# Attention scores on half of the array's rows: both halves beside each other, in four groups of four matmuls

## The reference, cut to what matters

```python
x = x + _L0_xattn_ref(_layernorm(x), ctx_1024, Wq, Wk, Wv, Wp, bp)   # x: (32, 256, 256), ctx: (32, 120, 256)
x = x + _L0_ffn_ref(_layernorm(x), ...)
# in _L0_xattn_ref, q = split(x @ Wq), k = split(y @ Wk), v = split(y @ Wv), 16 heads of 16:
attn = jnp.einsum('bhid,bhjd->bhij', q, k) * SCALE
attn = jax.nn.softmax(attn, axis=-1)
out = jnp.einsum('bhij,bhjd->bhid', attn, v)
...
return out @ Wp + bp
```

## Time and profile before

| what | value |
|---|---|
| median of 2 runs | 975.79 us (974.56 to 977.03) |
| the profiled execution, its own time | 970.46 us |
| its span | 968.7 us |
| PE, DVE, ACT, POOL busy, share of the span | 88%, 77%, 53%, 61% |
| mean granted clock of TensorE | 0.941 |

### The profile page before, as it was taken

How to read it: one execution, slowest core, us unless ns; L and a number is a source line. 1 busy time by engine, 2 the same in 40 slices (tenths; PEclk the granted TensorE clock), 3 DMA queues, 4 the chain that set the end, 5 groups by cost and what they waited for, 6 DMA issues and landing times. The chain is left out here.

```text
span 968.7 us, 20968 instructions
## 1 busy us (share of the span) xinstructions
PE 848.8 (88%) x6115; PEld 727.1 (75%) x6115; DVE 742.9 (77%) x1659; ACT 510.7 (53%) x929; POOL 594.6 (61%) x562
## 2 busy tenths in 40 slices
PE   8799999999999999998611149999999999999995
PEld 6578888878888888886501137989999999999985
DVE  5588888888888888876598856988777777777642
ACT  4555565556655665565165107465555555555531
POOL 4266666677666766666342255588887776775345
PEclk9999999999999999999755559999999999999998
DMA  5466566566665665554141033466666556665333
GB/s 173 162 226 213 195 213 221 201 199 213 226 204 195 211 225 201 195 189 143 65 145 44 8 104 118 136 198 171 165 168 162 157 159 162 159 174 149 97 72 43
DMA packets 129508, 156.49 MB, mean 162 GB/s; under 512 B 22448, under 2 KB 104624, under 8 KB 129344
## 3 DMA queue, kind: packets, MB, share of 16 engines
q1 hardware_dynamic: 104064, 113.05, 35.9%
q0 software_dynamic: 15616, 25.70, 12.3%
q10 hardware_dynamic: 9792, 17.31, 4.9%
HBM read 74.93 MB, written 26.28 MB: 104 GB/s over the span
## 5 line engine op out<-in xcount | busy, mean ns | idle before, releaser
L583 DVE TENSOR_REDUCE NM<-bank 128x4 f32<-128x480 f32 x256 | 155.4, 649 | 60.6 <-PE bank L741 60.5
L414 ACT ACTIVATE PT<-bank 120x512 f32<-120x512 f32 x256 | 142.8, 603 | 36.6 <-PE bank L766 35.4
L342 POOL TENSOR_SCALAR XN<-X,mv,rstd 128x256 f32<-128x256 f32 x124 | 150.9, 1226 | 14.2 <-POOL rstd L337 13.3
L1656 PE MATMUL bank<-W2H,HH 128*128 128x256 f32 x512 | 144.8, 283 | 2.0 <-issue 2.0
L1658 PE MATMUL bank<-W2H,HL 128*128 128x256 f32 x512 | 143.6, 280 | 0.0
L1657 PE MATMUL bank<-W2L,HH 128*128 128x256 f32 x512 | 143.5, 280 | 0.0
L1117 POOL DMA_INDIRECT out_dram<-C,IO x60 | 111.3, 1855 | 50.7 <-issue 31.0
L1385 DVE TENSOR_TENSOR HL<-hf,HH 128x512 fp32r<-128x512 f32 x128 | 87.3, 690 | 49.8 <-ACT HH L1540 49.1
L766 PE MATMUL bank<-QX,KX 128*120 128x256 f32 x512 | 110.0, 307 | 9.4 <-DMA QX<-NMT 5.7
L541 DVE RECIPROCAL RR<-RC 128x256 f32<-128x256 f32 x64 | 111.5, 1743 | 6.3 <-DMA RC<-PVS 6.3
L1535 ACT ACTIVATE hf<-bank,B 128x512 f32<-128x512 f32 x128 | 87.9, 687 | 40.6 <-PE bank L1658 34.9
(11 more groups left out here) (192 smaller groups left out, 1888.4 us busy)
## 6 DMA issues: line engine op xcount, KB each, us to landing
QX<-QH ACTq DMA_DIRECT2D x64, 256.0 KB
W<-w1T_dram SPq DMA_DIRECT2D x16, 1024.0 KB, 5.5
W<-w2T_dram SPq DMA_DIRECT2D x16, 1024.0 KB, 5.8
X<-x_dram SPq DMA_DIRECT2D x32, 256.0 KB, 3.2
QX<-QL SPq DMA_DIRECT2D x32, 256.0 KB
XB<-x_dram SPq DMA_DIRECT2D x32, 256.0 KB, 2.8
RC<-PVS SPq DMA_DIRECT2D x64, 128.0 KB, 2.1
OC<-PVS SPq DMA_DIRECT2D x64, 128.0 KB, 2.3
```

What stands on the lines that cost most here:

```text
L342: ins = pool.tensor_scalar(dst[:, t, :], src[:, t, :], mv[:, t, 0:1], rstd[:, t:t + 1], ALU.subtract, ALU.mult)
L414: act.activation(PT[u][0:M, HE * k:HE * (k + 1), :], score_bank(b, k // 2)[k % 2][0:M, :], ACT.Exp, scale=SCALE) \
L583: dve.tensor_reduce(NM[u][:, t, :].rearrange("p (f n e) -> p n e f", n=HN, e=HE)[:, n, :, :], smax_bank[q % 2][:, 0:4 * M].rearrange("p (e ...
L1656: pe.matmul(o, wh, xh, start=first, stop=False)
```

## The change

`scores(n)` now runs for n = 0 to 3. Each call issues four matmuls: for each of two heads e, both halves f, on partitions 0 to 63 and 64 to 127 of `KX` and `QX`, the first into one bank, the second into the other. It waits once, until both banks have been read. The semaphore of half f is raised at the matmul of e = 1. The order of TensorE's step is rewritten around the four calls. ScalarE's code is the same.

```diff
-            def scores(k):
+            def scores(n):
                 b, u, j, live = batch(i, c, 0)
                 if live:
-                    n, f = k // HALVES, k % HALVES
-                    if k == 0:
+                    if n == 0:
                         pe.wait_ge(max_moved[u], 16 * (j + 1))
-                    wait(pe, exp_ready, NX * b + (k - HALVES * (2 if n > 0 and known(b) and b == B - 1 else 1) + 1))
+                    wait(pe, exp_ready, NX * b + HALVES * (n - (1 if n > 0 and known(b) and b == B - 1 else 0)))
                     for e in range(HE):
-                        ins = pe.matmul(score_bank(b, n)[f][0:M, e * S:(e + 1) * S], KX[u][:, n, f, e, :],
-                                        QX[u][:, HE * n + e, :], start=True, stop=True)
-                    ins.then_inc(score_done, 1)
+                        for f in range(HALVES):
+                            rows = slice(HP * f, HP * (f + 1))
+                            ins = pe.matmul(score_bank(b, n)[f][0:M, e * S:(e + 1) * S], KX[u][rows, n, f, e, :],
+                                            QX[u][rows, HE * n + e, :], start=True, stop=True)
+                            if e == HE - 1:
+                                ins.then_inc(score_done, 1)
...
             scores(0)
-            scores(1)
             values()
             if first == -1:
                 warm_up(WARM[2])
+            max_scores(0)
+            scores(1)
+            max_scores(1)
+            rows2()
             scores(2)
-            max_scores(0)
-            scores(3)
-            max_scores(1)
-            scores(4)
-            rows2()
-            scores(5)
             rows()
             if last == 3:
                 turn_logits(1, 0, EARLY)
             max_scores(2)
-            scores(6)
             max_scores(3)
-            scores(7)
+            scores(3)
             weigh(0)
             weigh(1)
```

## The result

| what | before | after |
|---|---|---|
| median | 975.79 us (2 runs) | 1002.34 us (999.33 to 1005.35, 2 runs) |
| ratio | | 1.028, 95% interval 1.023 to 1.033 |
| the profiled execution, its span | 970.46, 968.7 us | 1005.35, 1003.6 us |

A forecast was written before the change was run, and what follows sets the result against it. In the edited stretch ACT's exponentials and their handover were taken to set the pace, though PE is busiest overall. 0.57 us a step over 31 steps gives 17.7 us, 975.79 to about 994 us; range 989 to 1013 us.

The forecast's parts named there:

- handover: From the end of a pair's last exponential through the next score matmuls to the next exponential: ACT idle 0.65 us.
- The round: One scores(n) and its pair of exponentials: 1.09 us of exponentials plus 0.65 us between pairs, 1.74 us.
- the 0.94 us: PE time saved per step as sixteen score matmul slots of 0.12 us become eight; forecast to end in PE's waits.
- the changes of tiling: Seven more switches a step around the score groups, each bounded between nothing and 0.2 us, mostly falling into waits.
- The step "scores(0)": First score group, behind the router's matmuls: 0.09 us of drain, exp(0) moving from 205.68 to 205.70.
- The step "scores(1)": Second score group: PE arrives about 206.78, exp(1) ends 206.79, exp(2) starts at 207.44 instead of 207.07.
- The path to the weighing: From exp(4) at 209.18 through scores(3) to weigh(0) at 210.77, which PE reaches 0.57 us later than before.
- 31 of the 32 steps have this form: Attention steps: each 0.57 us longer, 17.7 us in all; the last sequence, with four score banks, put at nothing.
- forecast A: Halves run beside each other, exponentials' round sets the pace: 0.45 to 0.75 us a step, 990 to 999 us, chance 0.70.
- rival B: Row tiles don't run beside each other, four slots per group: 34 to 37 us slower, 1010 to 1013 us, chance 0.15.
- Rival C: Switch to row tiles dearer than 0.2 us, felt around scores(0): 25 to 28 us slower, 1001 to 1004 us, chance 0.12.
- Rival D: PE's work is the price and waits cost nothing: 29 us gained, 947 us, chance 0.03.

The follow-up runs named there:

- The wait alone: Kernel before, order and full rows kept, each score call waiting until both banks of the pair are read: 1008.33 us, ratio 1.034, step 14.94 us.
- the cut exponentials: Half of each exponential left out in both kernels, 256 of 512 columns read: changed kernel 981.89 us, kernel before 969.39 us.

## Why the prediction was right, and where it was off

- **Sign and cause: right.** ACT's round of a pair and its handover set the pace, PE's saving was used up. The wait alone (1.14 us a step) and the cut exponentials (0.51 us more gained than in the kernel before) show it.
- **The round: right.** 1.74 us from the earlier trace rows; measured 1.76, and 1.79 where PE came late; 1.74 twice with max_scores(0) moved.
- **Where the 0.94 us went: in part wrong.** "The 0.94 us that it saved are in its waits", and of the changes of tiling "it matters little, as most switches fall into a wait". Seven of them cost 0.94 + 0.33 = 1.27 us, more than was saved, so PE's own work grew from 13.41 to 13.74 us. The sum along ACT's rounds came out all the same, as the changes ahead of the third and fourth group end before the exponentials do. With no wait for ACT at all the change would still be slower, by an estimated 0.33 us a step.
- **The step "scores(0)": too small.** I gave it 0.02 us on the assumption that a drain behind the router's matmul takes 0.10. The router's last matmul starts at 210.26 + 0.97 - 0.26 = 210.97, the scores' load at 211.16, 0.19 later, and exp(0) comes 0.10 later on average (the 0.18 of the one step have 0.08 of the projection's ups and downs in them).
- **The step "scores(1)": too small by 0.03 on average**, 0.05 in the step shown. "PE's margin here is all but nothing" was right, and it was used up: the load of max_scores(0), whose call waits for transfers, begins at 212.56, only when the values' last matmul has streamed.
- **The path to the weighing: right**, 1.56 us from exp(4) to the weighing's load, as foreseen (209.18 to 210.74).
- **Sum.** 0.57 us a step forecast, 0.69 measured, 17.7 against 21.4 us for 31 steps. "31 of the 32 steps have this form" left out the fill: about 6 us more lie in the first two steps and the sixth to eighth. Hence 994 forecast and 1002.3 measured, on the side of 2% that I gave 0.52. The step of 0.69 us lies in forecast A's own range of 0.45 to 0.75; the time lies outside its 990 to 999 us. That it is inside the whole range is luck in part: the upper end was set by rival B, which is out.
- **Rival B** (no rows beside each other) is out: a group's 0.50 us are 0.10 of load, one slot of 0.12 and one matmul of 0.28, so the halves run together. **Rival C** was right in its place, PE's margin ahead of scores(1), and wrong in its reason: a change cost 0.18 to 0.20, not above, and its 1001 to 1004 us came about through other terms. **Rival D** is out: with the waits for ACT taken off, the changes of tiling use up the saving and 0.33 us a step more.
- **The two rules.** The Trainium skill, TensorEngine Tiling (Array Packing), Key Properties, says that changing the tiling mode drains TensorE. The traces agree: 0.18 us each, seven times, more than the saving. The Trainium skill, same page, PSUM Bottleneck, says that the evacuation of PSUM may become the bottleneck when tiling speeds up TensorE. The traces agree here too: the waits for ACT grew by 0.36 us a step.
- **What would show it.** "PE's busy time should fall" was wrong: it rose from 13.50 to 13.82 us a step, since a matmul whose load is bare is recorded from the load on. A row's idle bracket also hides that part: PE's 0.38 us at 214.72 is 0.62 for the load itself.

## What to carry to other kernels

Before a consumer's two buffers are filled as a pair, look at who is dense in that very stretch, not over the step: one value of a semaphore cost 1.14 us in 13.8 with ACT 59% busy. Row tiles pay only where a group saves more than its two changes of tiling, here some 0.36 us against 0.24 us saved by four matmuls of 256 columns; where the tiling changes anyway it came out even, and longer groups were not tried. To find what a wait costs, shorten the consumer in both kernels and compare the differences, but look at the weight loads as well: a wait that is left there has no bracket on the matmul.

## What the runs showed of the hardware

- Two tiles of 64 rows run beside each other into two banks: four matmuls of 256 columns take the two slots of 0.12 us of a full-row pair.
- A change between full rows and 64-row tiles costs 0.18 to 0.20 us: 0.18 to 0.20 read off single pairs, 0.18 from thirteen changes in one run, 0.18 from seven in another. This is in line with what the column tiles showed before (0.09 to 0.10 of drain and a bare load of 0.10). Behind the router's last matmul of 16 columns the load came 0.19 us after that matmul's start, where it had come after 0.08 without a change.
- TensorE's granted clock was at its lower level, 1.2 GHz, for 17 us of the first 60 us in both profiles of the changed kernel, with PE busy 48.89 of those 60 us in the second; in the kernel before 7 us or none, with PE busy 50.17 and 49.09. It fell in the middle too: in the first profile to a mean of 0.55 between 120 and 125 us and of 0.66 between 140 and 145, behind waits of PE of 1.28 and 1.05 us for a transfer, and in the changed kernel with short exponentials to 0.69 between 135 and 140 us, behind one of 1.87 us. In the second profile it stayed at 1.00 behind waits of 1.15 and 0.78 us. Neither the busy time nor the one wait in the trace tells these apart; what does stays open.
